# A quantised feed-forward on one core: the products of the next token tile placed between the quantisation steps of this one, and the last tile in two parts

## The chip, the cores and the metric

The kernel runs on one core of a Trainium2 chip. Its time is device microseconds (us), the median of several timed executions. One more execution was taken with the hardware profiler, and the times of single instructions come from that one. The engines are TensorE (PE: matmuls and transposes; PEld is its weight load), VectorE (DVE), ScalarE (ACT), GpSimd (POOL), and the sync engine SP, which here only issues transfers. Each takes its instructions in program order; they wait for one another at semaphores.

## The reference

512 tokens (2 x 256) of width 512 go through four layers, each with a layer norm before it and a sum with its input behind it: an 8-bit quantised cross attention, a block-quantised feed-forward, a 32-head attention against a context, and a ternary feed-forward. The change is in the second:

```python
def _mx_quant(x, mbits):            # blocks of 32 along the last dim
    amax = jnp.max(jnp.abs(xb), axis=-1, keepdims=True)
    shared_exp = jnp.floor(jnp.log2(jnp.where(amax > 0, amax, 1.0))) - EMAX
    scale = jnp.exp2(shared_exp)
    q = _quant_elem(xb / scale, mbits) * scale

gate = _mx_linear(x, w_gate)        # quant_fp6(x) @ quant_fp4(w)^T
up = _mx_linear(x, w_up)
inter = jax.nn.silu(gate) * up      # 512 tokens x 1376
x = x + _mx_linear(inter, w_down)   # inter is quantised to fp6 first
```

## The kernel before, in words

The program is four stages one after another. From 0 to about 209 us the weights of the quantised feed-forward are quantised chunk by chunk on DVE and POOL and turned on PE, with the keys and values of the later attention computed beside them. Then comes the quantised feed-forward (about 209 to 258 us), a layer norm and the queries' start (to about 275 us), the 32-head attention (to about 687 us), and the last feed-forward.

In the quantised feed-forward the 512 tokens are four tiles of 128 (t = 0 to 3), and the 1376 inner columns are padded to 1408 and cut into slices of 512, 512 and 384 (c = 0, 1, 2; slice number n = 3t + c). A slice takes these steps:

- PE, `gate_up(t)` (L474): 4 matmuls for gate, 4 for up, into a pair of PSUM banks. There are two pairs, so slice n waits until the product of slice n-2 is made (`inter_ready`).
- ACT, `silu(t)` (L704): silu of the gate, into `silu0`, which has two halves.
- DVE, `inter_products(t)` (L1133): silu times up into `int0`.

Then the whole tile is quantised and multiplied:

- DVE, `fp6` (L1084 to L1089): the largest magnitude of each block of 32 (`f6_amax`), four small operations on the 44 results, and the scaled rounding into `f6` (L1089). `fp6_clip` (L1095, L1096): the scale back (`f6_e`) and the clip into `f6c`, one buffer, which waits until POOL has read the tile before.
- POOL, `fp6_out` (L849): `int_q`, the quantised values.
- PE, `turn_inter(t)` (L482): 11 transposes. ACT, `keep_inter(t)` (L709): their copy `int_T` to SBUF.
- PE, `down(t)` (L489): 11 matmuls. DVE, `add_down(t)` (L1142): the sum into `X`.

The order is written out by hand on each engine. PE: `gate_up(0)`, a weight turn (`mx_turn`, L411), `gate_up(1)`, the last weight turn, `turn_inter(0)`, then for t = 2 and 3 `gate_up(t)`, `down(t-2)`, `turn_inter(t-1)`, and at the end `down(2)`, `turn_inter(3)`, `down(3)`. ACT: for t = 2 and 3 `silu(t)`, `keep_inter(t-1)`. DVE: all three products of a tile, then all its quantisation steps, then (from t = 2) `add_down(t-2)`. After the last tile DVE adds `down(1)` and `down(2)` to `X`, makes the layer norm of tiles 0 to 2 in one go (`row_stats` L971, `normalise` L977 to L987), then adds `down(3)` and makes the norm of tile 3. PE turns the normalised rows (L511), and the queries of the attention follow (L579). POOL, after its last `fp6_out`, splits query weights in high and low parts (L886, L888).

Of the kernel before, what the change touches and what calls it, by code (L numbers as in the profile page):

```python
# [78 lines left out]
def build(nc, x, ctx_rows, ctx_cols, ctx_tiles, mask, scalars, ident, rope_k, rope_q, mxw, mxw_last,  # L79
          wk, wv, wq, wo, gate_w, up_w, down_w, k_scr, v_scr, out):  # L80
    with ExitStack() as ctx:
# [34 lines left out]
        with ExitStack() as a:  # L116
# [28 lines left out]
            with ExitStack() as b:  # L145
                silu0 = sb("silu0", [P, 2, 512], F32, b)
                int0 = sb("int0", [P, IPAD], F32, b)
                f6 = sb("f6", [P, NT * D], FP8, b)
                f6c = sb("f6c", [P, NT * D], BF16, b)
                int_q = sb("int_q", [P, 2, IPAD], BF16, b)  # L150
                int_T = sb("int_T", [P, 2, IPAD], BF16, b)
# [34 lines left out]


# [195 lines left out]
        def _(pe):  # L383
# [94 lines left out]
            def turn_inter(t):  # L478
                pe.wait_ge(intq_ready, t + 1)
                after(pe, intT_ready, t)  # L480
                for c in range(NI):
# [3 lines left out]
            def down(t):  # L485
                pe.wait_ge(intT_ready, t + 1)
                after(pe, ffn0_done, t - 1)
                for c in range(NI):
                    last = mm(bank(2 + t % 2), int_T[:, t % 2, c * P:(c + 1) * P], WT[:, 2 * NI + c], start=(c == 0), stop=(c == NI - 1))  # L489
# [8 lines left out]
            for t in range(2, NT):  # L498
                gate_up(t)
                down(t - 2)  # L500
                turn_inter(t - 1)
            down(NT - 2)
            turn_inter(NT - 1)
# [152 lines left out]
        def _(act):  # L656
# [49 lines left out]
            def keep_inter(t):  # L706
                act.wait_ge(intq_turned, t + 1)
                after(act, down_sums, t - 1)
                copy(int_T[:, t % 2], bank16(0, IPAD)).then_inc(intT_ready, 1)  # L709
# [9 lines left out]
            keep_inter(NT - 1)  # L719
# [98 lines left out]
        def _(pool):  # L818
# [46 lines left out]
            for i in range(NFULL - 1):  # L865
# [5 lines left out]
                if i == L0_AT + 1:  # L871
                    fp6_out(q1[:].rearrange("p t d -> p (t d)"), NT * D, 0, q1_ready)
# [86 lines left out]
        def _(dve):  # L959
# [121 lines left out]
            def fp6(src, n):  # L1081

                m = n // BLK
                chain(f6s, nc.vector.tensor_reduce(f6_amax[:, 0:m], blocks(src), AX.X, ALU.max, apply_absolute_value=True))  # L1084
                chain(f6s, ts(f6_amax[:, 0:m], f6_amax[:, 0:m], 2.0 ** -100, None, ALU.max))
                chain(f6s, ts(f6_amax[:, 0:m].bitcast(U32), f6_amax[:, 0:m].bitcast(U32), EXP_MASK, None, ALU.bitwise_and))
                chain(f6s, ts(f6_r[:, 0:m].bitcast(I32), f6_amax[:, 0:m].bitcast(I32), -1.0, float(0x7F000000), ALU.mult, ALU.add))
                chain(f6s, ts(f6_r[:, 0:m], f6_r[:, 0:m], 2.0 ** -4, None, ALU.mult))
                chain(f6s, tt(blocks(f6[:, 0:n]), blocks(src), over(f6_r[:, 0:m], m), ALU.mult, saturate=False))  # L1089

            def fp6_clip(n, earlier):
                m = n // BLK
# [13 lines left out]
            for i in range(NFULL - 1):  # L1106
# [222 lines left out]
```

## Time and profile before

| what | value |
|---|---|
| time, median of 3 runs (lowest to highest) | 795.27 us (794.51 to 795.56) |
| profiled execution: span, first to last instruction | 792.6 us |
| median less span: what lies around the span | 2.7 us |
| PE busy | 694.3 us (88% of the span) |
| DVE busy | 602.5 us (76%) |
| POOL busy | 497.3 us (63%) |
| ACT busy | 338.9 us (43%) |

The profiler gives its execution's span and no time beside it; the 2.7 us between that span and the median of the runs is taken as what lies around the span. Busy shares are means over the whole program, in which the long attention stage counts most. The stage that the change touches is some 50 us of it, and is to be read from its own instructions in order of time.

### The profile page before, as it was taken

How to read it: one execution, taken by the hardware profiler on the slowest of the kernel's cores; microseconds unless marked ns; L12 is line 12 of the kernel's file. 1: busy time of each engine (PE TensorE's matmuls, PEld its weight loads, DVE VectorE, ACT ScalarE, POOL GpSimd, SP SyncE). 2: the span in 40 equal slices, each digit the busy share in tenths (PEclk: the TensorE clock that was granted, in tenths of full speed). 3: DMA queues.
4: the chain of work that ended last, by engine and by line, in shares of the span. 5: the costliest groups of instructions: out<-in, count | busy, mean ns of one | idle time of the engine just before them, and what ended most of it. 6: DMA issues, size and time to landing. Idle time of an engine off the chain costs nothing.

```text
span 792.6 us, 10943 instructions
## 1 busy us (share of the span) xinstructions
PE 694.3 (88%) x3104; PEld 507.6 (64%) x3104; DVE 602.5 (76%) x1050; ACT 338.9 (43%) x654; POOL 497.3 (63%) x407
## 2 busy tenths in 40 slices
PE   4789638966676689999999999999999999599998
PEld 1344314433233567888888888888888888378886
DVE  6869999998878678888878878888888887631112
ACT  1323112212323267666666656666566665031111
POOL 0789897668424368675766667676767555517662
PEclk9979878978779899999999999999999999989999
DMA  8643432232140012212121221202111102202321
GB/s 336 249 142 124 133 119 74 73 106 66 54 146 26 26 54 94 67 54 67 40 93 39 80 66 40 93 26 93 44 62 58 36 27 93 62 19 81 118 79 53
DMA packets 38314, 65.67 MB, mean 83 GB/s; under 512 B 3344, under 2 KB 11664, under 8 KB 37264
## 3 DMA queue, kind: packets, MB, share of 16 engines
q1 hardware_dynamic: 38288, 65.36, 25.1%
q8 instruction: 12, 0.20, 0.1%
q14 instruction: 14, 0.11, 0.0%
HBM read 55.91 MB, written 9.44 MB: 82 GB/s over the span
## 4 chain that ended last, share of the span: by engine, by line
PE 64%; DVE 25%; issue 7%; POOL 2%; DMA 1%; ACT 1%; SPq 0%; POOLq 0%; DVEq 0%; ACTq 0%
PE ps L517 15%; PE ps L519 15%; PE ps L518 15%; PE ps L579 11%; PE ps L546 7%; DVE mx_q L1071 4%; DVE mx_m L1063 2%; DVE mx_q L1073 2%; DVE mx_amax L1048 2%; PE ps L474 2%; DVE mx_amax L1050 1%; DVE mx_raw L1069 1%; DMA k_scr<-k_cos 1%; DVE ctx_f L1000 1%; DVE k_cos L1079 1%
## 5 line engine op out<-in xcount | busy, mean ns | idle before, releaser
L897 POOL TENSOR_SCALAR prob<-prob,rinv 128x512 f32<-128x512 f32 x128 | 90.0, 703 | 122.1 <-DVE rinv L1203 122.1
L741 ACT ACTIVATE prob<-ps,nmax 128x512 f32<-128x512 f32 x128 | 88.4, 690 | 62.5 <-DVE nmax L1196 60.0
L579 PE MATMUL ps<-xt,wq_sb 128*128 128x512 f32 x384 | 106.4, 403 | 5.5 <-POOL wq_sb L888 2.2
L752 ACT CAST pT<-ps 128x512 fp32r<-128x512 f32 x128 | 75.1, 587 | 81.2 <-PE ps L546 80.3
L1196 DVE CUSTOM_DVE_ANT_0 ps<-ps,mask_sb 128x512 f32<-128x512 f32 x128 | 88.3, 690 | 18.2 <-PE ps L519 17.2
L1217 DVE TENSOR_TENSOR pT<-ps,pT 128x512 fp32r<-128x512 f32 x128 | 86.9, 679 | 4.7 <-ACT pT L752 1.7
L579 PEld LDWEIGHTS ps<-xt,wq_sb 128*128 128x128 f32 x384 | 73.9, 194 | 24.0 <-issue 4.6
L422 PE MATMUL ps<-ctxT,wk_sb 128*128 128x512 f32 x128 | 62.7, 647 | 18.2 <-DMA ctxT<-in_ctx_cols 10.5
L546 PE MATMUL ps<-idf,prob 128*128 128x128 f32 x512 | 76.6, 272 | 0.0
L546 PEld LDWEIGHTS ps<-idf,prob 128*128 128x128 f32 x512 | 64.0, 142 | 16.2 <-POOL prob L897 0.3
L432 PE MATMUL ps<-wv_sb,ctt 128*128 128x512 f32 x128 | 60.0, 624 | 16.3 <-DVE X L1036 16.3
L517 PE MATMUL ps<-pT,vt 128*128 128x512 f32 x128 | 61.1, 478 | 0.2 <-DVE pT L1217 0.2
L830 POOL TENSOR_TENSOR mx_raw<-mx_raw,mx_r 128x2048 f32<-128x2048 f32 (+1 forms) x9 | 44.0, 4889 | 27.0 <-DVE mx_r L1054 27.0
L422 PEld LDWEIGHTS ps<-ctxT,wk_sb 128*128 128x128 f32 x128 | 26.2, 209 | 50.6 <-issue 45.1
L432 PEld LDWEIGHTS ps<-wv_sb,ctt 128*128 128x128 f32 x128 | 25.6, 202 | 49.0 <-issue 31.8
L1248 DVE SCALAR_TENSOR_TENSOR int<-ps,sc,silu 128x512 f32<-128x512 f32 x11 | 8.3, 751 | 61.7 <-PE ps L519 61.7
L900 POOL TENSOR_TENSOR q_swp<-q_swp,ropeQ 128x512 f32<-128x512 f32 x32 | 41.4, 1293 | 19.1 <-ACT q_swp L762 18.5
L517 PE MATMUL ps<-wo_sb,oT 128*128 128x512 f32 x128 | 50.2, 392 | 2.2 <-DVE oT L1190 1.4
L1182 DVE TENSOR_TENSOR X<-ps,X 128x512 f32<-128x512 f32 x64 | 43.7, 682 | 10.6 <-PE ps L519 10.6
L519 PE MATMUL ps<-pT,vt 128*128 128x512 f32 x128 | 50.8, 397 | 0.0
L517 PE MATMUL ps<-kt,qt 128*128 128x512 f32 x128 | 50.0, 391 | 0.4 <-ACT prob L741 0.4
L518 PE MATMUL ps<-pT,vt 128*128 128x512 f32 x128 | 50.3, 393 | 0.0
(147 smaller groups left out, 1722.7 us busy)
## 6 DMA issues: line engine op xcount, KB each, us to landing
mx_raw<-in_mxw SPq DMA_DIRECT2D x8, 1024.0 KB, 6.2
wq_raw<-in_wq SPq DMA_DIRECT2D x32, 256.0 KB, 3.1
wo_raw<-in_wo SPq DMA_DIRECT2D x32, 256.0 KB, 2.6
k_scr<-k_cos SPq DMA_DIRECT2D x16, 256.0 KB, 6.3
v_scr<-v_st SPq DMA_DIRECT2D x16, 256.0 KB, 6.4
kr<-k_scr SPq DMA_DIRECT2D x16, 256.0 KB, 2.8
vr<-v_scr SPq DMA_DIRECT2D x16, 256.0 KB, 3.4
ffn_raw<-in_gate_w SPq DMA_DIRECT2D x11, 256.0 KB, 2.7
```

The source lines that it names most:

```text
L422: last = mm(bank(4 + b), wk_sb[:, p, k], ctxT[:, k, b * CTX:(b + 1) * CTX], start=(k == 0), stop=(k == KD - 1))
L432: last = mm(bank(6 + n), ctt[:, p, k], wv_sb[:, k, n * 512:(n + 1) * 512], start=(k == 0), stop=(k == KD - 1))
L517: mm(out_ap, left[0], right[0], start=first, stop=False)
L518: mm(out_ap, left[0], right[1], start=False, stop=False)
L519: return mm(out_ap, left[1], right[0], start=False, stop=final)
L546: last = nc.tensor.transpose(bank(2 + i % 2)[:, k * P:(k + 1) * P], prob[:, i, k * P:(k + 1) * P], idf[:])
L579: last = mm(query_bank(H), wq_sb[:, par, l, k], xt[:, r, k], start=(n == 0), stop=(n == 11))
L741: nc.scalar.activation(prob[:, j], bank(j % 2), ACT.Exp, bias=nmax[:, j:j + 1], scale=-1.0, accum_out=rsum[:, j:j + 1]).then_inc(exps, 1)
L752: copy(pT[:, v % 2, 0, :, i * P:(i + 1) * P], bank(2 + i % 2).rearrange("p (k c) -> p k c", k=4)).then_inc(ph_ready, 1)
L897: nc.gpsimd.tensor_scalar(prob[:, i], prob[:, i], rinv[:, i:i + 1], 1.0, ALU.mult, ALU.mult).then_inc(probs, 1)
L1196: nc.vector.tensor_tensor_reduce(out=bank(j % 2), in0=bank(j % 2), in1=mask_sb[:, 2 * (u % 2) + j % 2], scale=-1.0, scalar=BIG, op0=ALU.ad ...
L1217: tt(pT[:, v % 2, 1, :, i * P:(i + 1) * P], bank(2 + i % 2).rearrange("p (k c) -> p k c", k=4), pT[:, v % 2, 0, :, i * P:(i + 1) * P].bitc ...
```

## The change

`int0` gets two halves, one for each parity of t. `fp6` is split into `fp6_exponents` (the maxima and the four small operations) and `fp6_round`. On DVE the products of tile t+1 are no longer made together behind the clip of tile t: the first stands between exponents and round of tile t, the second between round and clip, the third behind the clip. The last tile is quantised in two parts, columns 0 to 1024 (its first two slices) and 1024 to 1408 (its third), each with its own exponents, round and clip on DVE, its own `fp6_out` on POOL, its own `turn_inter` on PE and its own `keep_inter` on ACT. On PE the first part's `turn_inter` stands ahead of `down(2)`, the second's behind it. The tile written `t` in `parts(t)` has one part except the last.

```diff
-                int0 = sb("int0", [P, IPAD], F32, b)
+                int0 = sb("int0", [P, 2, IPAD], F32, b)
...
+        def parts(t):
+
+            return [(0, 1024), (1024, IPAD)] if t == NT - 1 else [(0, IPAD)]
...
-            def turn_inter(t):
-                pe.wait_ge(intq_ready, t + 1)
+            def turn_inter(t, part=0):
+                lo, hi = parts(t)[part]
+                pe.wait_ge(intq_ready, t + part + 1)
                 after(pe, intT_ready, t)
-                for c in range(NI):
+                for c in range(lo // P, hi // P):
                     last = nc.tensor.transpose(bank16(0, IPAD)[:, c * P:(c + 1) * P], int_q[:, t % 2, c * P:(c + 1) * P], idb[:])
                 last.then_inc(intq_turned, 1)
 
             def down(t):
-                pe.wait_ge(intT_ready, t + 1)
                 after(pe, ffn0_done, t - 1)
-                for c in range(NI):
-                    last = mm(bank(2 + t % 2), int_T[:, t % 2, c * P:(c + 1) * P], WT[:, 2 * NI + c], start=(c == 0), stop=(c == NI - 1))
+                for part, (lo, hi) in enumerate(parts(t)):
+                    pe.wait_ge(intT_ready, t + part + 1)
+                    for c in range(lo // P, hi // P):
+                        last = mm(bank(2 + t % 2), int_T[:, t % 2, c * P:(c + 1) * P], WT[:, 2 * NI + c], start=(c == 0), stop=(c == NI - 1))
                 last.then_inc(down_sums, 1)
...
+            turn_inter(NT - 1, 0)
             down(NT - 2)
-            turn_inter(NT - 1)
+            turn_inter(NT - 1, 1)
             down(NT - 1)
...
-            def keep_inter(t):
-                act.wait_ge(intq_turned, t + 1)
+            def keep_inter(t, part=0):
+                lo, hi = parts(t)[part]
+                act.wait_ge(intq_turned, t + part + 1)
                 after(act, down_sums, t - 1)
-                copy(int_T[:, t % 2], bank16(0, IPAD)).then_inc(intT_ready, 1)
+                copy(int_T[:, t % 2, lo:hi], bank16(0, IPAD)[:, lo:hi]).then_inc(intT_ready, 1)
...
-            keep_inter(NT - 1)
+            keep_inter(NT - 1, 0)
+            keep_inter(NT - 1, 1)
...
-                fp6_out(int_q[:, t % 2], IPAD, t + 1, intq_ready)
+                for part, (lo, hi) in enumerate(parts(t)):
+                    fp6_out(int_q[:, t % 2, lo:hi], lo, hi, t + part + 1, intq_ready)
...
+            def fp6_exponents(src, lo, hi):
+
+                b, e = lo // BLK, hi // BLK
+                chain(f6s, nc.vector.tensor_reduce(f6_amax[:, b:e], blocks(src), AX.X, ALU.max, apply_absolute_value=True))
+                chain(f6s, ts(f6_amax[:, b:e], f6_amax[:, b:e], 2.0 ** -100, None, ALU.max))
+                chain(f6s, ts(f6_amax[:, b:e].bitcast(U32), f6_amax[:, b:e].bitcast(U32), EXP_MASK, None, ALU.bitwise_and))
+                chain(f6s, ts(f6_r[:, b:e].bitcast(I32), f6_amax[:, b:e].bitcast(I32), -1.0, float(0x7F000000), ALU.mult, ALU.add))
+                chain(f6s, ts(f6_r[:, b:e], f6_r[:, b:e], 2.0 ** -4, None, ALU.mult))
+
+            def fp6_round(src, lo, hi):
+                b, e = lo // BLK, hi // BLK
+                chain(f6s, tt(blocks(f6[:, lo:hi]), blocks(src), over(f6_r[:, b:e], e - b), ALU.mult, saturate=False))
+
+            def fp6_clip(lo, hi, earlier):
+                b, e = lo // BLK, hi // BLK
                 for s, count in earlier:
                     after(dve, s, count)
-                ts(f6_e[:, 0:m], f6_amax[:, 0:m], 2.0 ** 4, None, ALU.mult)
-                ts(f6c[:, 0:n], f6[:, 0:n], 7.5 / 64, -7.5 / 64, ALU.min, ALU.max).then_inc(f6_clipped, 1)
+                ts(f6_e[:, b:e], f6_amax[:, b:e], 2.0 ** 4, None, ALU.mult)
+                ts(f6c[:, lo:hi], f6[:, lo:hi], 7.5 / 64, -7.5 / 64, ALU.min, ALU.max).then_inc(f6_clipped, 1)
...
-            def inter_products(t):
-                for c, (lo, hi) in enumerate(bounds):
-                    n = 3 * t + c
-                    dve.wait_ge(silu_ready, n + 1)
-                    tt(int0[:, lo:hi], silu0[:, n % 2, 0:hi - lo], bank(5 + 2 * (n % 2), hi - lo), ALU.mult).then_inc(inter_ready, 1)
-
-            def inter_quantise(t):
-                dve.wait_ge(inter_ready, 3 * t + 3)
-                fp6(int0[:], IPAD)
-                fp6_clip(IPAD, [(q1_ready, 2), (intq_ready, t)])
+            def inter_product(t, c):
+                n, (lo, hi) = 3 * t + c, bounds[c]
+                dve.wait_ge(silu_ready, n + 1)
+                tt(int0[:, t % 2, lo:hi], silu0[:, n % 2, 0:hi - lo], bank(5 + 2 * (n % 2), hi - lo), ALU.mult).then_inc(inter_ready, 1)
 
             def add_down(t):
                 dve.wait_ge(down_sums, t + 1)
                 tt(X[:, t], bank(2 + t % 2), X[:, t], ALU.add).then_inc(ffn0_done, 1)
 
-            inter_products(0)
+            for c in range(3):
+                inter_product(0, c)
             mx_round(NFULL, 0, lambda: None)
-            inter_quantise(0)
-            inter_products(1)
-            inter_quantise(1)
-            for t in range(2, NT):
-                inter_products(t)
-                inter_quantise(t)
-                add_down(t - 2)
+            for t in range(NT - 1):
+                dve.wait_ge(inter_ready, 3 * t + 3)
+                fp6_exponents(int0[:, t % 2], 0, IPAD)
+                inter_product(t + 1, 0)
+                fp6_round(int0[:, t % 2], 0, IPAD)
+                inter_product(t + 1, 1)
+                fp6_clip(0, IPAD, [(q1_ready, 2), (intq_ready, t)])
+                if t >= 2:
+                    add_down(t - 2)
+                if t < NT - 2:
+                    inter_product(t + 1, 2)
+            for part, (lo, hi) in enumerate(parts(NT - 1)):
+                if part == 1:
+                    inter_product(NT - 1, 2)
+                dve.wait_ge(f6_clipped, NT)
+                dve.wait_ge(inter_ready, 3 * (NT - 1) + 2 + part)
+                fp6_exponents(int0[:, (NT - 1) % 2, lo:hi], lo, hi)
+                fp6_round(int0[:, (NT - 1) % 2, lo:hi], lo, hi)
+                fp6_clip(lo, hi, [(intq_ready, NT - 1)])
+            add_down(NT - 3)
             add_down(NT - 2)
             dve.wait_ge(ffn0_done, NT - 1)
             for t in range(NT - 1):
```

DVE, from the round of tile 0 to the products that belong to tile 2. L1133 (before) and L1147 (now) are the products `int0`, `f` is `f6`, L1096 and L1110 are the clip. Before:

```order
L1089 TENSOR_TENSOR f<-int,f_r 128x1408
L1095 TENSOR_SCALAR f_e<-f_amax 128x44
L1096 TENSOR_SCALAR f6c<-f 128x1408
L1133 TENSOR_TENSOR int<-silu,ps 128x512 x2
L1133 TENSOR_TENSOR int<-silu,ps 128x384
L1084 TENSOR_REDUCE f_amax<-int 128x44
L1085 TENSOR_SCALAR f_amax<-f_amax 128x44
L1086 TENSOR_SCALAR f_amax<-f_amax 128x44
L1087 TENSOR_SCALAR f_r<-f_amax 128x44
L1088 TENSOR_SCALAR f_r<-f_r 128x44
L1089 TENSOR_TENSOR f<-int,f_r 128x1408
```

And now, from the third product of tile 1 on:

```order
L1147 TENSOR_TENSOR int<-silu,ps 128x384
L1095 TENSOR_REDUCE f_amax<-int 128x44
L1096 TENSOR_SCALAR f_amax<-f_amax 128x44
L1097 TENSOR_SCALAR f_amax<-f_amax 128x44
L1098 TENSOR_SCALAR f_r<-f_amax 128x44
L1099 TENSOR_SCALAR f_r<-f_r 128x44
L1147 TENSOR_TENSOR int<-silu,ps 128x512
L1103 TENSOR_TENSOR f<-int,f_r 128x1408
L1147 TENSOR_TENSOR int<-silu,ps 128x512
L1109 TENSOR_SCALAR f_e<-f_amax 128x44
L1110 TENSOR_SCALAR f6c<-f 128x1408
```

The first two products of tile 2 stood behind the clip of tile 1; one of them now stands ahead of its round (L1103), the other ahead of its clip.

PE, the end of the stage: L482 (now L487) are the transposes of `turn_inter`, L489 (now L495) the matmuls of `down`. Before, `down(1)`, `turn_inter(2)`, `down(2)`, `turn_inter(3)`, `down(3)`:

```order
L489 MATMUL ps<-WT,int_T 128x512 x11
L482 MATMUL ps<-idb,int_q 128x128 x11
L489 MATMUL ps<-WT,int_T 128x512 x11
L482 MATMUL ps<-idb,int_q 128x128 x11
L489 MATMUL ps<-WT,int_T 128x512 x11
```

Now, with the waits at each:

```order
L495 MATMUL ps<-WT,int_T 128x512 [waits intT_ready]
L495 MATMUL ps<-WT,int_T 128x512 x10
L487 MATMUL ps<-idb,int_q 128x128 [waits intT_ready,intq_ready]
L487 MATMUL ps<-idb,int_q 128x128 x10
L487 MATMUL ps<-idb,int_q 128x128 [waits intT_ready,intq_ready]
L487 MATMUL ps<-idb,int_q 128x128 x7
L495 MATMUL ps<-WT,int_T 128x512 [waits intT_ready,ffn0_done]
L495 MATMUL ps<-WT,int_T 128x512 x10
L487 MATMUL ps<-idb,int_q 128x128 [waits intT_ready,intq_ready]
L487 MATMUL ps<-idb,int_q 128x128 x2
```

Eight transposes of tile 3, which wait for POOL's first part of it, now stand ahead of the eleven matmuls of `down(2)`; the other three stand behind them.

## Rows read from the trace of the kernel before

**Rows 1.** The page's chain that ended last, by engine

```profile
PE 64%; DVE 25%; issue 7%; POOL 2%; DMA 1%; ACT 1%; SPq 0%; POOLq 0%; DVEq 0%; ACTq 0%
```

**Rows 2.** Windows: stretch, us, busy per engine (PE, PEld, DVE, ACT, POOL), PEclk, DMA

```profile
300.00:684.00 384.00, 382.51 (x1915) 316.07 (x1915) 314.79 (x688) 236.57 (x504) 252.99 (x266) 1.00 0.19 60
227.00:229.00 2.00, 2.00 (x7) 0.64 (x5) 1.83 (x6) 1.33 (x1) 0.00 (x0) 0.50 0.91 307
230.00:231.00 1.00, 1.00 (x6) 0.40 (x4) 0.91 (x2) 0.54 (x1) 0.01 (x1) 0.86 0.96 313
257.00:258.00 1.00, 1.00 (x6) 0.44 (x5) 1.00 (x3) 0.00 (x0) 0.00 (x0) 0.71 0.43 164
```

**Rows 3.** Timeline, DVE: start us, us, instruction, [idle before, releaser]

```profile
217.66 0.19 DVE L1085 TENSOR_SCALAR f_amax<-f_amax 128x44 f32<-128x44 f32 x1
...
218.54 1.62 DVE L1089 TENSOR_TENSOR f<-int,f_r 128x1408 fp8e4<-128x1408 f32 x1
...
220.30 0.88 DVE L1096 TENSOR_SCALAR f6c<-f 128x1408 bf16<-128x1408 fp8e4 x1
221.10 1.27 DVE L1133 TENSOR_TENSOR int<-silu,ps 128x512 f32<-128x512 f32 x2
225.13 0.55 DVE L1133 TENSOR_TENSOR int<-silu,ps 128x384 f32<-128x384 f32 x1 [2.76 <-ACT silu L704]
225.72 1.62 DVE L1084 TENSOR_REDUCE f_amax<-int 128x44 f32<-128x1408 f32 x1
...
231.09 0.69 DVE L1133 TENSOR_TENSOR int<-silu,ps 128x512 f32<-128x512 f32 x1 [0.19 <-ACT silu L704]
```

**Rows 4.** DVE's waits, 209 to 264 us: us in total, times, longest

```profile
DVE int L1133 <- ACT silu L704: 8.7, 6, 2.8
```

**Rows 5.** Timeline, POOL, tiles 0, 1 and 3

```profile
221.26 2.56 POOL L849 TENSOR_TENSOR int_q<-f6c,f_e 128x1408 bf16<-128x1408 bf16 x1 [4.04 <-DVE f6c L1096]
230.99 2.56 POOL L849 TENSOR_TENSOR int_q<-f6c,f_e 128x1408 bf16<-128x1408 bf16 x1 [7.17 <-DVE f6c L1096]
...
248.99 2.56 POOL L849 TENSOR_TENSOR int_q<-f6c,f_e 128x1408 bf16<-128x1408 bf16 x1 [6.50 <-DVE f6c L1096]
```

**Rows 6.** Timeline, PE, from gate_up(1)'s third slice to down(3)

```profile
221.83 2.74 PE L474 MATMUL ps<-WT,q1T 128*128 128x384 bf16 x8 [4.57 <-DVE int L1133]
...
225.68 1.36 PE L482 MATMUL ps<-idb,int_q 128*128 128x128 bf16 x11 [0.68 <-ACT WT L679]
226.83 6.63 PE L474 MATMUL ps<-WT,q1T 128*128 128x512 bf16 x24
...
246.92 2.55 PE L489 MATMUL ps<-WT,int_T 128*128 128x512 bf16 x11 [1.42 <-ACT int_T L709]
251.60 0.79 PE L482 MATMUL ps<-idb,int_q 128*128 128x128 bf16 x11 [2.13 <-POOL int_q L849]
253.81 4.24 PE L489 MATMUL ps<-WT,int_T 128*128 128x512 bf16 x11 [1.43 <-ACT int_T L709]
```

**Rows 7.** Timeline, ACT

```profile
230.47 0.60 ACT L704 ACTIVATE silu<-ps 128x512 f32<-128x512 f32 x1 [2.06 <-PE ps L474]
...
252.43 1.33 ACT L709 COPY int_T<-ps 128x1408 bf16<-128x1408 bf16 x1 [5.56 <-PE ps L482]
```

**Rows 8.** Timeline, DVE, the end of the stage

```profile
248.75 1.44 DVE L1142 TENSOR_TENSOR X<-ps,X 128x512 f32<-128x512 f32 x2
...
252.49 1.00 DVE L980 TENSOR_SCALAR var_eps<-meanvar 128x3 f32<-128x3 f32 x1
...
254.31 1.12 DVE L984 TENSOR_TENSOR newton<-newton,var_eps 128x3 f32<-128x3 f32 x1
...
258.21 0.69 DVE L1142 TENSOR_TENSOR X<-ps,X 128x512 f32<-128x512 f32 x1
...
262.01 0.55 DVE L987 TENSOR_SCALAR xhat<-X,meanvar,rstd 128x512 f32<-128x512 f32 x1
```

**Rows 9.** Timeline, POOL beside Rows 8

```profile
252.21 1.26 POOL L888 TENSOR_TENSOR wq_sb<-wq_raw,wq_sb 128x512 fp32r<-128x512 f32 x1
```

More of the change, by code:

```diff
@@ L844, in scale_out, with fp6_out @@
                 tt(blocks(mx_w[:, p, 0:n]), blocks(mx_q[:, p, 0:n]), over(mx_e[:, p, 0:n // BLK], n // BLK), ALU.mult).then_inc(mx_ready, 1)
-            def fp6_out(dst, n, turn, done):
+            def fp6_out(dst, lo, hi, turn, done):
                 pool.wait_ge(f6_clipped, turn + 1)
-                tt(blocks(dst), blocks(f6c[:, 0:n]), over(f6_e[:, 0:n // BLK], n // BLK), ALU.mult).then_inc(done, 1)
+                m = (hi - lo) // BLK
+                tt(blocks(dst), blocks(f6c[:, lo:hi]), over(f6_e[:, lo // BLK:hi // BLK], m), ALU.mult).then_inc(done, 1)
             def key_sine(i):
@@ L871, in _ @@
                 if i == L0_AT + 1:
-                    fp6_out(q1[:].rearrange("p t d -> p (t d)"), NT * D, 0, q1_ready)
+                    fp6_out(q1[:].rearrange("p t d -> p (t d)"), 0, NT * D, 0, q1_ready)
             key_sine(NFULL - 1)
@@ L1079, in key_cosine @@
                     tt(k_cos[:, b], bank(4 + b), ropeK[:, 0], ALU.mult).then_inc(k_cosed, 1)
[L1081 to L1092, printed above, removed]
+            def fp6_exponents(src, lo, hi):
[10 more added lines that the diff above has]
+                b, e = lo // BLK, hi // BLK
                 for s, count in earlier:
                     after(dve, s, count)
-                ts(f6_e[:, 0:m], f6_amax[:, 0:m], 2.0 ** 4, None, ALU.mult)
-                ts(f6c[:, 0:n], f6[:, 0:n], 7.5 / 64, -7.5 / 64, ALU.min, ALU.max).then_inc(f6_clipped, 1)
+                ts(f6_e[:, b:e], f6_amax[:, b:e], 2.0 ** 4, None, ALU.mult)
+                ts(f6c[:, lo:hi], f6[:, lo:hi], 7.5 / 64, -7.5 / 64, ALU.min, ALU.max).then_inc(f6_clipped, 1)
             def round_chunk(i):
@@ L1119, in _ @@
                     dve.wait_ge(ln_ready, 2 * NT)
-                    fp6(rows(xhat[:]), NT * D)
-                    fp6_clip(NT * D, [])
+                    fp6_exponents(rows(xhat[:]), 0, NT * D)
+                    fp6_round(rows(xhat[:]), 0, NT * D)
+                    fp6_clip(0, NT * D, [])
             key_cosine(NFULL - 1)
```

## The prediction

> **What bounds the kernel now.** I read the page's chain first. PE carries 64% of it and DVE 25% [rows 1]. The windows place the two: from 300 to 684 us PE is busy 382.5 of 384 us at full clock [rows 2], so the attention can neither wait out a late start nor profit beyond an early one. A shift at its entry should reach the end one for one. The DVE share lies before it. Then I read the timeline of the stage that the change touches, engine by engine, asking at each wait who came last.
>
> In tiles 0 and 1 DVE hardly rests: exponents, round and clip take 1.62 + 4 x 0.21 + 1.62 + 1.0 = 5.1 us a tile, the products 1.8 us more. The hole is the 2.76 us ahead of the third product, which waits for silu [rows 3]. It is a round trip: gate_up's third slice waits until the first product frees its banks, starts at 221.83 and takes 2.74 us for 8 matmuls [rows 6]. DVE's waits for silu make 8.7 us in all, up to 2.8 each [rows 4]; tile 0 has one of the longest, and without it tiles 1 to 3 hold about 6.0 us. The other engines have slack: POOL waits 4 to 7 us for each clip [rows 5].
>
> At the end two things finish together. down(3) ends at 253.81 + 4.24 = 258.05 [rows 6], and DVE, which made the norm of tiles 0 to 2 meanwhile, adds it at 258.21 [rows 8]. From there to the last normalised row, 262.56, is 4.35 us in line.
>
> **The change, step by step.** Each step is a time of the profiled clock; a semaphore costs 0.05 us.
>
> Tile 0. Two products now stand ahead of its clip: 1.27 us for two [rows 3], so 1.3. The clip's end moves from 221.2 to 222.5, and POOL's int_q(0) ends at 222.55 + 2.56 = 225.1. The first product, now at 218.5, releases gate_up(1)'s last slice at 219.2 in place of 221.8; the 2.76 us hole goes. The last weight copy too is early (by 223.2), so turn_inter(0), which began at 225.68 behind that copy [rows 6], now waits for POOL and begins at 225.15: 0.5 us earlier. That is all PE gains.
>
> Tile 1, the core of the forecast. DVE makes its third product and its exponents by 225.9, then stands at the first product of tile 2. That needs silu, which needs gate_up(2), which stands on PE behind turn_inter(0): 225.15 + 1.36 for the transposes + 8 matmuls at the lower clock, 0.427 each, 3.4, + silu 0.65 = 230.55. Before, silu began at 230.47 [rows 7] and DVE had nearly no wait (0.19 us [rows 3]), because it rounded and clipped tile 1 during this time, up to 230.9, just ahead of int_q at 230.99 [rows 5]. Now both are queued behind the waiting product: DVE idles some 4.6 us, then product 0.66, round 1.65, product 0.66, scale and clip 1.0: 234.5 in place of 230.9, +3.6. Behind them wait POOL, turn_inter(1), gate_up(3).
>
> Tile 2. The same circle at the higher clock: POOL 2.6 to 237.15; turn_inter(1) 0.8 (PE is there at 235.5 and waits); 8 matmuls at 0.23 (2.55 us for 11 of the same size [rows 6]) 1.85; silu 0.65 to 240.45; product, round, product, clip 4.0: 244.4. A circle is 9.9 us where DVE's own work was 9.0 a tile (int_q starts at 230.99 and 248.99, two tiles apart [rows 5]). The old order had POOL, PE and ACT work beside DVE's next tile; the new one puts all four in a row.
>
> Last tile. add_down(0) 0.7; exponents of 1024 columns: 1.62 x 1024/1408 = 1.2 to 246.3. The first small operation then meets POOL's int_q(2), 244.5 to 247.05. A small tensor_scalar beside POOL is held until POOL's instruction ends: var_eps takes 1.00 us where its like takes 0.19 [rows 3, 8], and ends at 253.49 with L888's 253.47 [rows 9]. So 247.1, + 0.65 for the rest, round 1.2, clip 0.75: 249.7. POOL's first part, 2.56 x 1024/1408 = 1.86: 251.6. What the split wins shows here: this is where all of int_q(3) ended before (251.55). The second part costs DVE 0.55 product, 0.5 maxima, again a wait for POOL, 0.65, 0.5, 0.4 to 252.9; POOL ends 253.7.
>
> PE's end. down(2), which ran 246.92 to 249.47 in a hole [rows 6], now stands behind the first part's transposes and so behind POOL at 251.6. Transposes 0.9 (8 at the lower clock) to 252.5. The clock: PE will have idled 3.8 us by then. In the trace it was at the lower level after a wait of 4.57 us (221.83, 0.34 us a matmul of 384), and at 253.81 after 0.79 us of work between waits of 2.13 and 1.43 [rows 6]; a window at 0.71 and one at 0.86 put its rises at about 257.6, 3.8 us into that burst, and at about 230.3, 4.6 us after turn_inter(0) began [rows 2, 6]. With 3.8 us from 251.6, down(2) has 7 matmuls at 0.427 and 4 at 0.23: 3.9 us, to 256.4. With none raised it is 4.7.
>
> DVE's end. The norm of tiles 0 to 2 waits for down(2). Before, it took from 249.51, when add_down(2) began (the second of the two adds [rows 8]), to add_down(3) at 258.21: 8.7 us. Of this 2.2 was waiting for POOL's weight splits (var_eps 0.85, rstd 0.4, newton 0.96 [rows 8]). The splits follow int_q, 253.7 to 257.6, and the norm's small operations come at 259.4, so the waits go: 6.5 us. add_down(3) starts at 256.4 + 0.05 + 6.5 = 262.95. down(3) is done by 259.4 and no longer decides. 262.95 less 258.21 is +4.7.
>
> The sum: +1.3 (clip 0), +2.3 (circle 1) and +1.0 (circle 2) make +4.6 at clip 2, 244.4 for 239.8. The last tile in parts gives this back: from clip 2 to POOL's first part it is 7.2 us, where to the whole int_q(3) it was 11.8, -4.6. From there to add_down(3) it was 258.21 - 251.55 = 6.7 and is now 0.9 + 3.9 + 6.55 = 11.35, +4.7. In all +4.7: span 797.3, and with the 2.7 us around it 800.0, which is the median of the runs, 795.27, plus 4.7.
>
> Costs not shown. int0's second half costs nothing: the instructions have the same sizes. No transfer is added or moved. Whether exponents of t+1 (1.62 us of reading, one input) slow beside POOL no row shows exactly: between nothing and the 0.4 of a held small operation a tile; I take nothing for the reduction, and the hold where it falls.
>
> The Trainium skill (SBUF — State Buffer, "SBUF: two separate sides") goes further: the port pair that VectorE and GpSimd share is locked for a whole instruction, for VectorE operations in a two-port mode and for those with two SBUF inputs. The trace agrees for the small operations; the round L1089 has two such inputs, and lies clear of POOL in both orders, so the rule adds nothing to the sum. Without any lock the sum would be about 0.5 less, 799.5.
>
> The Trainium skill (TensorE: Matmul & The Clock Gate, "Part 1: The HAM clock gate") has the array's clock halve after idling and return only after sustained work. It speaks against this change, which makes a wait ahead of down(2). The trace agrees, with 4.24 us for down(3) at 253.81 beside 2.55 for down(2). By it alone, with the return only behind down(2), the sum would be +5.5, 800.8.
>
> **Rivals.** A, the forecast: the waits of DVE at the first product of tiles 2 and 3, and down(2) late: +3.5 to +5.7, by when the clock rises inside down(2) (3 to 4.7 us) and inside gate_up(2).
>
> B, the end at the higher clock: the transposes at 251.60 ran high after 2.13 us of waiting [rows 6]. Then they take 0.6, and down(2) 2.6: +2.9, 798.2. Against it: the wait is 3.8 us here, and 253.81 was low.
>
> C, the higher clock comes later: after 221.83 it had not risen at 229 [rows 2], over 7 us on, with a break of 0.68 us. If gate_up(2)'s second slice and down(3) are low too, down(3) ends at 261 or later and circle 1 grows by 1: +5.6 to +8, 801 to 803.
>
> D, PE never falls after 219: gate_up(2) starts its circle with 0.8 + 1.85 us in place of 1.36 + 3.4, 2.1 less; with B's 1.8 less at the end 4.7 - 3.9 = +0.8, 796.1. Against it: PE waits 4.3 us ahead of turn_inter(0), as long as ahead of 221.83, where it fell.
>
> E, the other side: faster. If silu of the next tile is ready when DVE comes to its product, the 6.0 us of holes vanish and nothing takes their place: clip 3 ends 6.0 earlier, less 0.9 for POOL's hold (twice 2.6 for int_q less 2.2 for product and maxima) and 1.3 for the six small operations that the second part adds (6 x 0.21): -3.8, 791.5. It decides at one point: silu of slice 6 before 226, when DVE is there. For it: the third slice of tile 1 does come 2.6 us earlier. Against it: slice 6 stands on PE behind turn_inter(0), and that behind int_q(0), which can't end before 225; transposes, 8 matmuls and silu then take 3.3 us even at the higher clock.
>
> **Chances.** A 0.70, B 0.08, C 0.10, D 0.05, E 0.07. A measurement of this kernel tells 0.2%, 1.6 us, from no change. A, B and C are slower by more: 0.88. D is within: 0.05. E is faster: 0.07. The range leaves out D, E and the end of C, some 0.16: 797.2 to 802.5.
>
> **What would show it.** In the profile of the changed kernel: an idle of 4 to 5 us ahead of DVE's first product of tile 2, released by ACT's silu, and one of 2 to 2.5 us at tile 3's; POOL's int_q at about 222.6, 234.6, 244.5, then 249.8 and 253.0; turn_inter(0) released by POOL, not by the weight copy; down(2) behind the first part's transposes, with a matmul of over 0.3 us on average; var_eps short, 0.2 us; the last normalised row at about 267. The forecast is wrong if silu of slice 6 comes before 227, if down(2) ends before 254, or if the attention takes back part of the shift.

## The result and the profile after

The changed kernel takes 797.9 us in the median of 9 runs (796.19 to 800.92), the kernel before, on the same chip, 795.28 us (9 runs, 794.18 to 796.01). The ratio is 1.0044 with a 95% interval of 1.003 to 1.0059: slower by 2.4 to 4.7 us. It is not the ratio of the two medians, which is 1.0033 (that of the means is 1.0043): the nine runs of the changed kernel lie in two groups, and the median is the highest of the lower one. The profiled execution of the changed kernel took 800.8 us with a span of 799.0 (1.8 us lie around it), so it is one of the long ones of the nine; the mean granted clock sorts them: the four of 799.5 us and more had 0.936 to 0.940, the five of 797.9 and less 0.944 to 0.949. What it shows is read with that in mind.

The page's chain is within a point of what it was [rows 1]:

```profile
PE 63%; DVE 25%; issue 8%; POOL 2%; DMA 1%; ACT 1%; SPq 0%; DVEq 0%; POOLq 0%; ACTq 0%
```

The windows of the changed kernel, columns as in [rows 2]: first the stretch of down(2), in which the clock rose only near the end, at about 257.0, then the microsecond in which the clock rose in gate_up(2), at about 229.7.

```profile
252.50:257.20 4.70, 4.70 (x15) 1.77 (x13) 1.45 (x4) 1.01 (x1) 3.57 (x5) 0.52 0.00 0
229.00:230.00 1.00, 1.00 (x4) 0.39 (x3) 0.00 (x0) 0.18 (x1) 0.00 (x0) 0.64 0.93 354
```

DVE's timeline, with the rows that answer to [rows 3] and [rows 8]:

```profile
222.18 0.55 DVE L1147 TENSOR_TENSOR int<-silu,ps 128x384 f32<-128x384 f32 x1
222.77 1.62 DVE L1095 TENSOR_REDUCE f_amax<-int 128x44 f32<-128x1408 f32 x1
224.43 0.51 DVE L1096 TENSOR_SCALAR f_amax<-f_amax 128x44 f32<-128x44 f32 x1
...
230.52 0.69 DVE L1147 TENSOR_TENSOR int<-silu,ps 128x512 f32<-128x512 f32 x1 [4.92 <-ACT silu L711]
231.13 1.62 DVE L1103 TENSOR_TENSOR f<-int,f_r 128x1408 fp8e4<-128x1408 f32 x1
...
240.31 0.69 DVE L1147 TENSOR_TENSOR int<-silu,ps 128x512 f32<-128x512 f32 x1 [2.60 <-ACT silu L711]
...
250.76 0.93 DVE L1096 TENSOR_SCALAR f_amax<-f_amax 128x12 f32<-128x12 f32 x1
...
257.35 0.69 DVE L1151 TENSOR_TENSOR X<-ps,X 128x512 f32<-128x512 f32 x1 [3.37 <-PE ps L495]
...
260.34 0.17 DVE L991 TENSOR_SCALAR var_eps<-meanvar 128x3 f32<-128x3 f32 x1
...
263.88 0.68 DVE L1151 TENSOR_TENSOR X<-ps,X 128x512 f32<-128x512 f32 x1
...
267.66 0.55 DVE L998 TENSOR_SCALAR xhat<-X,meanvar,rstd 128x512 f32<-128x512 f32 x1
```

DVE's waits from 209 to 270 us, which answer to [rows 4]:

```profile
DVE int L1147 <- ACT silu L711: 10.3, 3, 4.9
DVE X L1151 <- PE ps L495: 3.4, 1, 3.4
```

Where six waits made 8.7 us, three now make 10.3, and a wait for PE (L495 is down) has come in. The old hole ahead of tile 1's third product is gone (222.18, no wait), but the first product of tile 2 (230.52) stood 4.92 us for silu with the round (231.13) queued behind it; tile 3's stood 2.60 us. POOL, for [rows 5]:

```profile
222.34 2.56 POOL L859 TENSOR_TENSOR int_q<-f6c,f_e 128x1408 bf16<-128x1408 bf16 x1 [5.24 <-DVE f6c L1110]
234.44 2.56 POOL L859 TENSOR_TENSOR int_q<-f6c,f_e 128x1408 bf16<-128x1408 bf16 x1 [9.54 <-DVE f6c L1110]
244.30 2.56 POOL L859 TENSOR_TENSOR int_q<-f6c,f_e 128x1408 bf16<-128x1408 bf16 x1 [7.29 <-DVE f6c L1110]
249.76 1.91 POOL L859 TENSOR_TENSOR int_q<-f6c,f_e 128x1024 bf16<-128x1024 bf16 x1 [2.90 <-DVE f6c L1110]
```

The old int_q(2), which [rows 5] leaves out, was:

```profile
239.93 2.56 POOL L849 TENSOR_TENSOR int_q<-f6c,f_e 128x1408 bf16<-128x1408 bf16 x1 [6.38 <-DVE f6c L1096]
```

int_q(1) begins 3.5 us later than before, int_q(2) at 244.30 where the old one began at 239.93, and the first part ends at 251.67, where the whole of int_q(3) had ended at 251.55. PE, for [rows 6], and ACT, for [rows 7]:

```profile
219.16 2.46 PE L478 MATMUL ps<-WT,q1T 128*128 128x384 bf16 x8 [2.22 <-DVE int L1147]
...
225.04 1.33 PE L487 MATMUL ps<-idb,int_q 128*128 128x128 bf16 x11 [2.99 <-POOL int_q L859]
...
251.72 1.03 PE L487 MATMUL ps<-idb,int_q 128*128 128x128 bf16 x8 [4.03 <-POOL int_q L859]
252.55 4.76 PE L495 MATMUL ps<-WT,int_T 128*128 128x512 bf16 x11
```

```profile
229.82 0.60 ACT L711 ACTIVATE silu<-ps 128x512 f32<-128x512 f32 x1 [2.08 <-PE ps L478]
```

turn_inter(0) (225.04) is now released by POOL, and 0.64 us earlier than before; slice 6's silu (229.82) gains those 0.65 us and no more. down(2) (252.55) takes 4.76 us at a granted clock of 0.52; it had taken 2.55. The norm of tiles 0 to 2 starts behind it, var_eps (260.34) is short, and the last normalised row ends at 268.21, 5.65 us later than 262.56 before. The rest of the span's +6.4 comes behind it, at the queries' start: their first matmuls begin 5.8 us later (270.24 for 264.43), those at 287.21 6.4 us later (280.81 before), and from there the shift stays.

### The profile page after: what moved, and what is told of

Same layout as the page of the kernel before. It is cut to its first block, busy times and chain, and to the rows that moved or that the text cites. A ratio compares the mean times of both kernels' runs of the same rounds, so it can differ in the third digit from the quotient of the medians.

```text
span 799.0 us, 10963 instructions
## 1 busy us (share of the span) xinstructions
PE 695.1 (87%) x3104; PEld 508.0 (64%) x3104; DVE 604.0 (76%) x1058; ACT 338.4 (42%) x655; POOL 497.3 (62%) x408
## 4 chain that ended last, share of the span: by engine, by line
PE 63%; DVE 25%; issue 8%; POOL 2%; DMA 1%; ACT 1%; SPq 0%; DVEq 0%; POOLq 0%; ACTq 0%
PE ps L524 15%; PE ps L526 15%; PE ps L525 15%; PE ps L586 10%; PE ps L553 7%; DVE mx_q L1082 4%; DVE mx_m L1074 2%; DVE mx_q L1084 2%; DVE mx_amax L1059 2%; DVE mx_amax L1061 1%; DVE mx_raw L1080 1%; DMA k_scr<-k_cos 1%; DVE ctx_f L1011 1%; DVE f L1103 1%; PE ps L478 1%
## 5 line engine op out<-in xcount | busy, mean ns | idle before, releaser
L426 PE MATMUL ps<-ctxT,wk_sb 128*128 128x512 f32 x128 | 60.8, 630 | 16.7 <-DMA ctxT<-in_ctx_cols 10.0
L524 PE MATMUL ps<-pT,vt 128*128 128x512 f32 x128 | 60.7, 474 | 0.2 <-DVE pT L1240 0.2
L526 PE MATMUL ps<-pT,vt 128*128 128x512 f32 x128 | 50.8, 397 | 0.0
L526 PE MATMUL ps<-kt,qt 128*128 128x512 f32 x128 | 50.5, 395 | 0.0
L524 PE MATMUL ps<-kt,qt 128*128 128x512 f32 x128 | 50.0, 391 | 0.5 <-ACT prob L750 0.5
```

Of the source, the lines that this page charges most:

```text
L426: last = mm(bank(4 + b), wk_sb[:, p, k], ctxT[:, k, b * CTX:(b + 1) * CTX], start=(k == 0), stop=(k == KD - 1))
L524: mm(out_ap, left[0], right[0], start=first, stop=False)
L526: return mm(out_ap, left[1], right[0], start=False, stop=final)
```

## The experiments

Ratios are to the kernel before on the same chip, with their 95% intervals. The kernels were timed on several chips, so two rows are compared by their ratios. In the expectations, theory T is the account that the prediction gave. L numbers are of each kernel's own text. "Last row" is the end of the last normalised row in the profiled execution (before 262.56, changed 268.21).

| kernel | ratio | last row |
|---|---|---|
| changed kernel | 1.0044 (1.003 to 1.0059) | 268.21 |
| down(2) first | 1.0032 (1.002 to 1.0044) | 264.97 |
| products alone | 1.0035 (1.0022 to 1.0049) | 264.29 |
| parts alone | 1.0000 (0.9991 to 1.0009) | 262.16 |
| PE's hole at the end filled | 1.0024 (1.0015 to 1.0034) | 264.92 |
| both holes filled | 1.0016 (1.0004 to 1.0029) | 263.82 |
| changed, gate_up ahead | 0.9971 (0.996 to 0.9982) | 260.71 |
| the same, last tile whole | 0.9917 (0.9899 to 0.9934) | 257.69 |
| again, another chip | 0.9932 (0.9913 to 0.9951) | 256.79 |
| gate_up ahead alone | 1.0005 (0.999 to 1.0021) | 263.26 |

### One part of the change at a time

**Products alone.** The last tile in one part, PE's and ACT's end as before:

```diff
-            return [(0, 1024), (1024, IPAD)] if t == NT - 1 else [(0, IPAD)]
+            return [(0, IPAD)]
...
-                if t < NT - 2:
-                    inter_product(t + 1, 2)
+                inter_product(t + 1, 2)
```

> Only the products of the next tile between the quantisation steps, the last tile whole, PE's and ACT's end as before. Theory T: clip 1 ends 3.4 us and clip 2 4.4 us later than before, as in the changed kernel; the whole int_q(3) begins at about 250.3 and ends at 252.9, +1.4 on before (two products of tile 3 no longer stand ahead of it); the last normalised row +1.5 to +2.5 us: ratio 1.002 to 1.003. Rival R2 (the products' new places gain, the parts lose): ratio below 1.000, up to 3.8 us faster. Idle of DVE ahead of tile 2's first product: T 4 to 5 us, R2 under 1 us.

```profile
233.94 2.56 POOL L857 TENSOR_TENSOR int_q<-f6c,f_e 128x1408 bf16<-128x1408 bf16 x1 [8.91 <-DVE f6c L1108]
243.78 2.56 POOL L857 TENSOR_TENSOR int_q<-f6c,f_e 128x1408 bf16<-128x1408 bf16 x1 [7.29 <-DVE f6c L1108]
250.13 2.56 POOL L857 TENSOR_TENSOR int_q<-f6c,f_e 128x1408 bf16<-128x1408 bf16 x1 [3.79 <-DVE f6c L1108]
```

1.0035, just above T's 1.002 to 1.003, with T's upper end inside the interval; the last row came 1.7 us late, as T had it. The clips are late nearly as in the changed kernel (POOL's rows 233.94 and 243.78, where 234.44 and 244.30 stood), and DVE waited 4.3 us at tile 2's first product and 2.6 at tile 3's.

**Parts alone.** The products of a tile together behind the clip again, the last tile in parts, with tile 3's third product between the parts:

```diff
                 fp6_exponents(int0[:, t % 2], 0, IPAD)
-                inter_product(t + 1, 0)
                 fp6_round(int0[:, t % 2], 0, IPAD)
-                inter_product(t + 1, 1)
                 fp6_clip(0, IPAD, [(q1_ready, 2), (intq_ready, t)])
                 if t >= 2:
                     add_down(t - 2)
+                inter_product(t + 1, 0)
+                inter_product(t + 1, 1)
```

> Only the last tile in parts (with PE's order of the changed kernel, down(2) behind the first part's transposes); the products of a tile together behind the clip, as before, except tile 3's third product, which stands between the parts. Theory T: clips 0 to 2 where they were before (221.1, 230.8, 239.7); the first part's int_q begins at about 245.2, the second's at about 248.9; down(2) starts at about 247.8 and ends by 250.3 to 252; last normalised row -0.6 us to +1: ratio 0.999 to 1.0015. Rival R1 (the parts are the loss): ratio 1.003 or more.

```profile
247.98 0.62 PE L487 MATMUL ps<-idb,int_q 128*128 128x128 bf16 x8 [2.45 <-POOL int_q L859]
248.44 2.54 PE L495 MATMUL ps<-WT,int_T 128*128 128x512 bf16 x11
```

1.0000. Here down(2) (248.44, L495) stands behind the first part's transposes too, but POOL's part is there at 247.9 and the clock is high: 2.54 us, and the place costs nothing. The parts came 0.8 us later than I had expected (int_q at 246.02 and 249.72), and the last row is 0.4 us earlier than before. So the loss of the change is made by the products' places; the parts, in this order, cost nothing that the times show.

### What the place of down(2) costs, and what the clock

**down(2) first.**

```diff
-            turn_inter(NT - 1, 0)
             down(NT - 2)
+            turn_inter(NT - 1, 0)
             turn_inter(NT - 1, 1)
```

> The changed kernel with one move on PE: down(2) stands ahead of the first part's transposes of tile 3 again. Theory T (DVE's in-order wait for silu costs until clip 2, and down(2) behind POOL costs at the end): down(2) ends at about 251.7 instead of 257.3, the norm of tiles 0 to 2 then starts behind DVE's own clips at about 254, meets POOL's weight splits again (held some 1 us), and the last normalised row comes some 1.3 to 2.5 us earlier than in the changed kernel: ratio to the kernel before 1.002 to 1.003 (+1 to +2.5 us). POOL's int_q times stay as they are in the changed kernel (222.3, 234.4, 244.3, 249.8). Rival R1 (the last tile's extra small operations are the loss, the place of down(2) is nothing): no difference from the changed kernel, ratio 1.0044. Rival R2 (down(2)'s place is all of the loss): ratio 1.000 or below.

```profile
225.07 0.78 PE L487 MATMUL ps<-idb,int_q 128*128 128x128 bf16 x11 [2.76 <-POOL int_q L859]
...
248.34 4.85 PE L495 MATMUL ps<-WT,int_T 128*128 128x512 bf16 x11 [1.51 <-ACT int_T L717]
```

```profile
253.23 0.69 DVE L1151 TENSOR_TENSOR X<-ps,X 128x512 f32<-128x512 f32 x1 [0.18 <-PE ps L495]
...
256.22 1.04 DVE L991 TENSOR_SCALAR var_eps<-meanvar 128x3 f32<-128x3 f32 x1
```

1.0032 beside 1.0044: just above the expected 1.002 to 1.003, and the intervals overlap, so the runs do not prove a gain. The profile shows how one would come: add_down(2) at 253.23 in place of 257.35, part of which is given back, since var_eps (256.22, 1.04 us) is again held by POOL's weight split. down(2) ran low here as well (4.85 us from 248.34), which I had expected to be high: it ended at 253.2, not at 251.7. In this execution turn_inter(0) ran high (225.07, 0.78 us) and int_q(1) began 0.9 us earlier, so not all of the 3.2 us to the changed kernel's last row belong to the move.

**PE's holes filled** with matmuls that nobody reads, first the one at the end, then also the one ahead of turn_inter(0):

```diff
+            pe.wait_ge(inter_ready, 3 * NT - 1)
+            for _ in range(16):
+                mm(bank(4), idb[:], WT[:, 0], start=True, stop=True)
             turn_inter(NT - 1, 0)
             down(NT - 2)
```

> The changed kernel with 16 extra matmuls (128x512, identity by weights, into a bank that nobody reads) in PE's 4 us hole between turn_inter(2) and the first part's transposes of tile 3; its output is unchanged. Theory T with the clock as a term of its own: the clock stays high, the eight transposes take 0.6 in place of 1.0 us and down(2) 2.6 in place of 4.8 us; the last normalised row comes 1.5 to 2.5 us earlier than in the profile of the changed kernel, and its runs lie closer together than the 796.2 to 800.9 there: ratio 1.001 to 1.003. Rival R3 (the clock is not it, down(2) is late only by its place): down(2) as long as before, ratio 1.0044 or, since the extra work delays the transposes, more.

```profile
246.54 3.62 PE L510 MATMUL ps<-WT,idb 128*128 128x512 bf16 x16
250.73 0.62 PE L487 MATMUL ps<-idb,int_q 128*128 128x128 bf16 x8 [0.57 <-POOL int_q L862]
251.19 2.54 PE L495 MATMUL ps<-WT,int_T 128*128 128x512 bf16 x10
```

The second kernel has this too:

```diff
             mx_turn(NFULL, 0)
+            pe.wait_ge(inter_ready, 5)
+            for _ in range(9):
+                mm(bank(4), idb[:], WT[:, 0], start=True, stop=True)
```

> As the kernel with 16 extra matmuls at the end, and nine more between the last weight turn and turn_inter(0), where PE has a hole of 3 us; output unchanged. Theory T: turn_inter(0) takes 0.8 and the first slice of gate_up(2) 1.85 us (1.33 and 3.4 in the changed kernel), so silu of that slice ends near 228.5, DVE's idle ahead of tile 2's first product shrinks from 4.9 to about 3 us but stays, and the end comes some 1 to 2 us earlier again: ratio 0.999 to 1.002. It does not reach the kernel with the reordering (0.9971), because the circle POOL, PE, ACT, DVE stays in line even at the high clock. Rival (DVE's idle is made by the clock alone): the idle falls under 1 us and the ratio under 0.998.

```profile
225.21 0.77 PE L487 MATMUL ps<-idb,int_q 128*128 128x128 bf16 x11 [0.57 <-POOL int_q L865]
```

```profile
228.44 0.69 DVE L1153 TENSOR_TENSOR int<-silu,ps 128x512 f32<-128x512 f32 x1 [2.68 <-ACT silu L717]
```

With the end filled (246.54), the transposes take 0.62 and down(2) 2.54 us; the ratio is 1.0024 (its interval just overlaps the change's), and the runs lie within 795.5 to 798.3. The last row is 3.3 us earlier than in the changed kernel's profile, but 1.0 of this was there before the filled hole: int_q(1) began at 233.45 for 234.44. With both filled turn_inter(0) takes 0.77, and DVE's wait falls from 4.92 to 2.68 us but stays: 1.0016, with an interval clear of the change's. So the clock makes part of the long down(2) and of DVE's idle, by the profiles, and the rival that it makes all of the idle is out. How much of the time it makes is not settled. The ratios put it at 0.28% of the 0.44%, but the two intervals are only 0.0001 apart, and the medians alone (1.0033 for the change, 1.0026 and 1.0029 for the two kernels here) show hardly a gain, and none from the second filling.

### The wait taken away, and what that needs

**gate_up ahead.** The changed kernel, with silu of the next tile no longer behind this tile's transposes (ACT likewise ahead of keep_inter):

```diff
             mx_turn(NFULL, 0)
+            gate_up(2, (0, 1))
             pe.wait_ge(mx_kept, NCH)
             turn_inter(0)
-            for t in range(2, NT):
-                gate_up(t)
-                down(t - 2)
-                turn_inter(t - 1)
+            gate_up(2, (2,))
+            down(0)
+            gate_up(3, (0, 1))
+            turn_inter(1)
+            gate_up(3, (2,))
+            down(1)
+            turn_inter(2)
```

> The changed kernel, with PE and ACT reordered so that silu of the next tile does not stand behind the transposes of this one: gate_up's first two slices of tile 2 stand ahead of turn_inter(0), those of tile 3 ahead of turn_inter(1), the third slices behind; silu likewise ahead of keep_inter. Theory T: DVE's idle of 4.9 us ahead of tile 2's first product and of 2.6 us ahead of tile 3's fall under 0.5 us each, int_q(1) begins at about 229.5 (234.4 in the changed kernel), int_q(2) at about 237, the first part at about 242.5; the last normalised row 6 us earlier than in the changed kernel and 1.5 to 2.5 us earlier than before: ratio 0.997 to 0.998. Rival R1 (parts and clock are the loss): ratio 1.002 or more.

```profile
DVE X L1160 <- PE ps L496: 3.4, 1, 3.4
DVE int L1156 <- ACT silu L717: 2.8, 1, 2.8
```

```profile
229.47 2.56 POOL L868 TENSOR_TENSOR int_q<-f6c,f_e 128x1408 bf16<-128x1408 bf16 x1 [4.66 <-DVE f6c L1119]
236.75 2.56 POOL L868 TENSOR_TENSOR int_q<-f6c,f_e 128x1408 bf16<-128x1408 bf16 x1 [4.72 <-DVE f6c L1119]
```

```profile
244.18 1.03 PE L488 MATMUL ps<-idb,int_q 128*128 128x128 bf16 x8 [4.02 <-POOL int_q L868]
245.00 4.81 PE L496 MATMUL ps<-WT,int_T 128*128 128x512 bf16 x11
```

0.9971. The waits of tiles 2 and 3 are gone (the 2.8 us left are tile 0's), and int_q(1) and (2) begin 5.0 and 7.5 us earlier than in the changed kernel. The last row is 7.5 us earlier than there and 1.9 us earlier than before (expected 6, and 1.5 to 2.5). DVE now waits 3.4 us for down(2), which stands behind a hole of 4.02 us (244.18) and runs 4.8 us.

> A second look at the kernel with the reordering of PE and ACT and the parts as in the change: theory T has DVE's idles ahead of the products of tiles 2 and 3 gone in this execution too, and down(2), behind a hole of 4 us, with a duration between 2.6 and 4.8 us by where the clock rises.

```profile
245.06 3.85 PE L496 MATMUL ps<-WT,int_T 128*128 128x512 bf16 x11
```

The same program, but the clock rose earlier, at about 247.7 us where it was 249.6 above: down(2) takes 3.85 us, and the one run 790.23 us.

**The same with a whole last tile**, and with it `down(2)` ahead of `turn_inter(3)` as before, twice:

> The previous kernel's reordering of PE and ACT (the next tile's gate_up and silu ahead of this tile's transposes and copy), with the products between the quantisation steps, but the last tile whole, and down(2) ahead of turn_inter(3) as before. Theory T: clips 0 to 2 as with the reordering and the parts (int_q at 222.3, 229.5, 236.8); the whole int_q(3) begins at about 243 and ends at about 245.7; down(2) runs in PE's hole ahead of it at about 241; the last normalised row is 1 to 2.5 us earlier than with the parts, 3.5 to 5 us earlier than before: ratio 0.994 to 0.996. Rival (the parts gain something at the end once DVE no longer waits): ratio 0.997 or more.

> The kernel with both (products between the steps, PE and ACT reordered) and a whole last tile, timed again beside the reordering alone: theory T 0.991 to 0.995.

```profile
243.54 2.56 POOL L866 TENSOR_TENSOR int_q<-f6c,f_e 128x1408 bf16<-128x1408 bf16 x1 [3.79 <-DVE f6c L1117]
```

```profile
242.11 2.53 PE L496 MATMUL ps<-WT,int_T 128*128 128x512 bf16 x11 [1.51 <-ACT int_T L722]
...
248.46 4.42 PE L496 MATMUL ps<-WT,int_T 128*128 128x512 bf16 x10 [1.51 <-ACT int_T L722]
```

```profile
244.68 0.69 DVE L1158 TENSOR_TENSOR X<-ps,X 128x512 f32<-128x512 f32 x1 [0.69 <-PE ps L496]
...
248.87 1.12 DVE L1002 TENSOR_TENSOR newton<-newton,var_eps 128x3 f32<-128x3 f32 x1
...
253.34 0.69 DVE L1158 TENSOR_TENSOR X<-ps,X 128x512 f32<-128x512 f32 x1 [0.50 <-remote]
```

787.55 and 789.64 us, ratios 0.9917 and 0.9932: faster than the kernel before and the changed one, and in the first faster than I had expected. The rows are of the first. add_down(2) begins at 244.68, 5.2 us earlier than with the parts, since down(2) (242.11) runs in a hole ahead of POOL's int_q(3) and at the higher clock. The norm is held by POOL's weight splits again (248.87, 1.12 us), and then waits 0.5 us at 253.34. The profile names no engine for this wait; add_down(3) needs down(3), which ran low here (4.42 us from 248.46 for ten of its eleven matmuls; the record of the last is missing). In the second execution down(3) took 2.53 us and the wait was gone. Once DVE no longer waits for silu, the kernel with the parts is 0.4 to 0.5% slower than the one without. Two things differ between them, the parts and the place of down(2) behind the first part; no run separates them, and the profiles put the cost at down(2).

**gate_up ahead alone**, with DVE's order of before:

> The kernel before with only PE's and ACT's reordering (gate_up and silu of the next tile's first two slices ahead of this tile's turn_inter and keep_inter); DVE's products together behind the clip, the last tile whole. Theory T: no gain by itself, because DVE still makes the first product of a tile only behind the clip and gate_up's third slice still waits for it: int_q at about 221.3, 231, 240, 249 as before, ratio 0.999 to 1.001. Rival R4 (PE's order was the fault all along and the products' places do nothing): ratio 0.992 to 0.996, as with both.

```profile
230.79 2.56 POOL L866 TENSOR_TENSOR int_q<-f6c,f_e 128x1408 bf16<-128x1408 bf16 x1 [7.16 <-DVE f6c L1117]
```

```profile
231.36 2.74 PE L479 MATMUL ps<-WT,q1T 128*128 128x384 bf16 x8 [2.55 <-DVE int L1154]
```

```profile
234.66 0.56 DVE L1154 TENSOR_TENSOR int<-silu,ps 128x384 f32<-128x384 f32 x1 [2.76 <-ACT silu L716]
```

1.0005, no gain. DVE makes the first product of a tile behind the clip, so the third slice of gate_up (231.36), which waits for this product, comes late, and DVE waits 2.76 us for its silu (234.66). One half of the rearrangement alone costs (1.0035), the other alone gives nothing (1.0005); together they give 0.992 to 0.993.

## Why the prediction was right, and where it was off

The direction and the range held: 797.9 us in 797.2 to 802.5, slower. The forecast of +4.7 us was too large against +2.6 in the medians and +3.5 by the ratio; the profiled execution, at 800.8 us, is nearer to it. The mechanism of the DVE part is shown term by term below. That the median fell inside the range is in part luck: it lies 0.7 us above the lower end, and nearer to the 798.2 of rival B than to the forecast. The profile is of one of the long runs, and what the end looks like in a middle one no trace shows.

- Tile 0 and circle 1: forecast +3.6 at clip 1, measured +3.5 (int_q 234.44 for 230.99), with DVE's idle 4.92 us where 4.6 was said. That the products' places make it is shown: with them alone the kernel is about as slow as with all (1.0035 and 1.0044, intervals overlap), without them it is even, and with silu brought ahead the idle goes and the time falls below before.
- Circle 2: forecast +1.0, measured +0.9 (244.30 for 239.93 is +4.4 in all).
- The last tile in parts: -4.6, measured -4.25 (251.67 for 251.55). It gives back, as said. Alone it brings nothing; the likely reason, read from the profile and not tested, is that the end of the stage runs through DVE's own work and norm and not through int_q's end.
- down(2): forecast 3.9 us, measured 4.76. I had the clock rise 3.8 us after 251.6, taken from one burst; here it rose at about 257.0, 5.3 us after 251.7. The prediction had this case too: 4.7 us with no rise inside down(2), and 800.8 us in all. That this is the profiled execution's time is chance in part, because the span also grew behind the last row. The term varies: 4.76 and, with gate_up ahead, 4.81 and 3.85 in two executions of one program; 2.54 where the hole is filled. The same stretch of program ran differently higher up as well: turn_inter(0) took 1.33 us in the changed kernel's profile and 0.78 with down(2) first. I had priced one phase of it as if each run had it, and a median over runs gives less. That this is what separates the median from the forecast is likely from the clocks of the nine runs, not shown run by run.
- The norm without POOL's hold: forecast 6.5 us, measured 263.88 - 257.35 = 6.53.
- Behind the last row the prediction had the shift go through one for one. It grew from 5.65 to 6.4 us at the queries' start, a term that was put at nothing; from there to the end of the span it stayed.
- The 2.7 us around the span was wrong: it is 1.8 in all nine runs of the changed kernel, so 792.6 was the span of an execution below the median. The sum was saved from it only by being set on the median too.
- Three sums were off by 0.1 to 0.3 us without changing a chance. B takes 0.3 us off the transposes and 1.3 off down(2), so its +2.9 should be +3.1 and D's +0.8 should be +1.0. The terms for the second part's clip add to 253.15, not 252.9; it ended at 253.4, and nothing waited for it that the sum needs.
- Of the rivals, E named the right condition (silu of slice 6 ready when DVE comes) and was out here, since it came at 230.4. With the condition made true and the parts kept, its -3.8 us was too much: the medians give -1.9 and the ratio -2.3, since down(2) still came late, a term that E left out. The kernel with the whole last tile gains 5.2 to 6.8 us; that this is near E's 6.0 us of holes is no test of it, because there down(2) has moved too. B, C and D price other phases of the clock. They may be the spread of the runs rather than rivals; with one profile of the changed kernel that is not shown.

## What to carry to other kernels

Before an instruction is moved ahead on an in-order engine, follow what it waits for through the other engines' orders: here DVE's product moved ahead, while silu for it still stood behind this tile's transposes on PE, and work that had run side by side became a ring of four engines. Here the move paid only when it was made on all engines of the ring at once: DVE's half alone cost 0.35%, PE's and ACT's half alone gave nothing, both gained 0.7 to 0.8%. And a hole on PE was not only idle time: behind some of them the matmuls ran at half the clock for 3.5 us in one execution and 5.4 us in another of the same program (from 244.2 us on, with gate_up ahead).

## What the runs showed of the hardware

A small DVE operation on operands in SBUF beside a POOL tensor_tensor ended with it in each case looked at: 224.43 + 0.51 = 224.94 (its like takes 0.19) with POOL's int_q(0) at 222.34 + 2.56 = 224.90, and 0.93 us at 250.76, to 251.69, beside the first part, which ended at 251.67. A DVE tensor_reduce that ran wholly beside int_q(0) (222.77) kept its 1.62 us, which answers what the prediction left open.

A PE hole of 2.99 us was followed by transposes at the lower clock in one execution (1.33 us for 11) and one of 2.76 us by transposes at the higher in another (0.78); what the PE had done in the 10 us before did not differ by more than 0.3 us in start or length. The windows of the two executions, the changed kernel first:

```profile
220.00:229.00 9.00, 6.01 (x28) 3.16 (x26) 5.39 (x10) 2.34 (x3) 2.56 (x1) 0.50 0.62 194
```

```profile
223.00:226.00 3.00, 0.93 (x13) 0.84 (x14) 2.46 (x6) 0.11 (x1) 1.93 (x1) 1.00 0.81 274
227.00:229.00 2.00, 2.00 (x6) 0.72 (x5) 0.00 (x0) 0.30 (x2) 0.00 (x0) 0.50 0.88 279
```

With down(2) first the clock stood at the higher level from 223 to 226, while PE was mostly idle, and was back at the lower one from 227 to 229, in the middle of matmuls; in the changed kernel it stayed low all through. So here the level did not follow at once from whether PE was busy, and a price for the clock taken from one execution is good for a median only as a range.
